# A graph layer kernel: W1's last half in two parts, the node table's rows laid by partitions, a shortened passage and written-out layers

## The chip, the cores and the metric

The kernel runs on one core of a Trainium2 chip. The metric is the device time of one execution in microseconds; lower is better. The time before is 4889.76 us, the median of three runs (4889.51 to 4896.31). The granted TensorE clock of the profiled execution was 0.958 of full speed on average.

## The reference, cut to what matters

The program is one GPS layer on a graph with N = 6250 nodes of 256 features and E = 100000 edges, sorted by destination. Six GNN layers follow one another; then comes a small attention-like term and a feed-forward stage with eight experts.

```python
xn = _layernorm(x, axis=-1)
h = xn
for layer in range(6):                                   # the GNN
    agg = jax.ops.segment_sum(h[src], dst, num_segments=n)
    z = h + agg
    z = z @ W1[layer] + b1[layer]
    z = relu(batchnorm(z, g1[layer], be1[layer]))        # mean and variance over all nodes
    z = z @ W2[layer] + b2[layer]
    z = batchnorm(z, g2[layer], be2[layer])
    h = z if layer == 5 else relu(z)
x = x + h + mix(xn)                                      # 8 heads, k and v normed, kv = k'v / N
x = x + ffn(_layernorm(x))                               # 8 experts: 3 products each, mixed by a softmax
```

Each batch norm needs the mean and the variance over all 6250 nodes, so no row of the next product can start before the last row of the one before is known. Each gather `h[src]` needs the whole table of h. These are the barriers of the program.

## The kernel before, in words

**Data.** 6250 nodes are padded to 6272 = 49 tiles of 128, in NC = 7 chunks of CT = 7 tiles (CN = 896 columns, halves of HN = 448). The state lives transposed in SBUF as `Zt` (features on partitions, nodes as columns, FB = 2 blocks of features). A copy of it by rows lies in DRAM as `y_table` (6272 x 256 fp32, 1 KB a row). Node t*128+p is row t*128+p of it (`y_t`, L102), so a chunk of 7 tiles goes to and from SBUF in pieces of 1 KB.

**Edges.** The 784 tiles of 128 edges are cut into S = 7 sections of 112. The first 50 tiles of each section are gathered: GpSimd issues one indirect DMA for each tile (`gather`, L654) that fetches 128 rows by `idx`. The other 62 are summed by a dense product with an adjacency block, that is built in the first layer and kept in DRAM (`dense_half`, L904). In layers 1 to 5 there are 350 gathers each, in 91 quads of up to four tiles. ScalarE and VectorE split a quad into high and low terms (`quad_high` L1140, `quad_low` L1391), TensorE multiplies it with one-hot matrices (`quad`, L809), VectorE sums a group of quads (`group_rows`, L1487), TensorE transposes it (L817) and VectorE adds it into a window of 128 columns of `Zt` (`add_group`, L1500). Four quads of gathered rows are in flight, so gather n waits until quad n-4 is multiplied. The dense halves lie between the quads in an order written out by hand (`halves_at`, with PRE = 6 halves ahead of the first quad).

**W1.** `w1_half` (L928) multiplies one half chunk (448 columns) with W1. In layers 1 to 5 thirteen of the 14 halves lie among the last quads. The 14th, the first half of chunk 6, waits for the last group and comes after it. ScalarE copies each result back to `Zt` (`evict_z1`, L1160) and VectorE takes its statistics from there (`z1_stats`, `half_stats`, L1519).

**The passage** is what lies between the last gather of a layer and the first of the next:

1. the last group, W1's last half, its eviction and statistics;
2. `bn_coefficients` on VectorE (two `bn_aggr` L1608, then seven small steps L1609 to L1617, each waiting for the one before, with a square root on ScalarE, L1165, in between);
3. ScalarE's `affine` (L1115) of the first half chunk, and `w2_stage` on TensorE: 14 halves, 112 matmul records (L967), evicted by ScalarE (L1174), statistics by VectorE (L1519);
4. `bn_coefficients` again;
5. `rows_of_h`: ScalarE's affine with Relu over all columns (the first chunk in pieces of 4 and 3 tiles), TensorE's transposes (L786), VectorE's 28 copies (`copy_rows`, L1378) into three row buffers `Rb`, and SP's stores to `y_table` (`store_rows`, L512: one for a chunk, two for the last). A copy of chunk c waits until chunk c-3 is stored. GpSimd's `table_complete` holds the first gather until all stores have landed. VectorE then makes the low terms of the first chunk (L1384), and TensorE starts the dense halves with them.

**Loops.** On all engines layer 0 is written out and layers 1 to 5 are one hardware loop over l (`with pe.Fori(1, L)`, `act.Fori`, `dve.Fori`, `pool.Fori`; SP's has l = 1 to 4 and one more). VectorE's loop starts with `layer_parameters` (L1630) and ends with the second `bn_coefficients`. The feed-forward stage runs seven chunks of eight experts; chunks 0 to 5 are a hardware loop on TensorE, ScalarE, GpSimd and VectorE. In each expert step TensorE does two times seven products (`hidden`, L1064) and 28 output products (`outputs`, L1073), VectorE adds products (L1827) and outputs (L1843), and GpSimd forms sums of weights and inputs and adds a biased row for each of seven tiles (L735). At a chunk's last expert it puts `chunk_inputs` (L707 to L713: rel, rest, idx as buffers for the next chunk's inputs) behind its third row.

**The start.** Until about 96 us the kernel norms x, stores the table (ScalarE's queue, seven chunks) and `xn_cols`, and VectorE computes the edge tables in a chain of steps, each waiting for the one before (L1653 to L1741). A flag at its end says whether edges are left for `general_pass`, a slow path that doesn't run with these inputs. The first gather waits for the flag.

```python
W1_ORDER = [*range(HALVES - 2), HALVES - 1, HALVES - 2]      # HALVES = 14
last_ = sections(gb_f)[:, S - 1, 0:GS // PJ]                 # no group of the last section reaches chunk 6's second half
step(tsc(last_, last_, float((NC - 1) * CN + HN - P), None, ALU.min))
```

## Time and profile before

| | us |
|---|---|
| median of 3 runs | 4889.76 (4889.51 to 4896.31) |
| the profiled execution: its own time | 4891.97 |
| its span, first to last instruction | 4889.9 |
| TensorE matmul busy | 4457.0 (91%) |
| GpSimd busy | 3100.2 (63%) |
| VectorE busy | 3051.6 (62%) |
| ScalarE busy | 2636.4 (54%) |
| start until the first gather | 98.3 |
| first gather of layer 0 to first gather of layer 1 | 883.2 |
| first gather of layer 1 to that of layer 5 | 2293.8, or 573.4 a layer |
| first gather of layer 5 to the end of the span | 1614.6 |

Busy shares are means over stages that have different limits. How to read it: the stages repeat, so one layer (here the one whose first gather is at 1554.99 us and whose successor's is at 2128.84 us) is read in full and the others are compared with it. The timelines give for each group of instructions its start, its length in us, engine, source line, operation, tiles and, in brackets, how long its engine stood idle before it and what ended that.

### The profile page before, as it was taken

To read this page: it belongs to the slowest core of one execution; us is meant where nothing else is said; L and a number is where in the kernel's file an instruction comes from. 1 tells how busy PE (TensorE), PEld (TensorE's weight loads), DVE (VectorE), ACT (ScalarE), POOL (GpSimd) and SP (SyncE) were. 2 spreads that over 40 slices of the span, in tenths; PEclk is the share of its full clock that TensorE was granted. 3 is DMA by queue.
4 is the path that set the end of the run, shared out by engine and by line. 5 is a ranking of instruction groups with operands and counts; after the bars stand their busy time and mean duration, and the time that the engine had idled before them with its cause. 6 is when DMAs were issued, how large, how long until landed. Compare 5 with 4: busy or idle time off the path is not lost.

```text
span 4889.9 us, 73690 instructions
## 1 busy us (share of the span) xinstructions
PE 4457.0 (91%) x18751; PEld 3229.0 (66%) x18751; DVE 3051.6 (62%) x6933; ACT 2636.4 (54%) x3302; POOL 3100.2 (63%) x3400
## 2 busy tenths in 40 slices
PE   3899999899987999889997999879998899999999
PEld 2666688477755878467774777547774766666665
DVE  6788766456664666556665566646665566666666
ACT  2677533555645655355555555455564355555555
POOL 1777765077761777447772677717775067777786
PEclk6999999999998999899999999989999899999999
DMA  5444653155533554255542555335555100000000
GB/s 196 135 150 155 218 154 96 63 158 170 157 103 106 167 165 149 65 161 166 159 131 77 166 165 160 113 101 161 164 152 169 60 10 9 9 9 9 9 8 8
DMA packets 248726, 560.54 MB, mean 115 GB/s; under 512 B 44210, under 2 KB 124956, under 8 KB 248156
## 3 DMA queue, kind: packets, MB, share of 16 engines
q0 software_dynamic: 109728, 299.78, 20.8%
q1 hardware_dynamic: 125788, 226.99, 14.1%
q10 hardware_dynamic: 12768, 28.90, 1.6%
q8 instruction: 153, 2.51, 0.2%
q14 instruction: 289, 2.37, 0.2%
HBM read 481.66 MB, written 73.84 MB: 114 GB/s over the span
## 4 chain that ended last, share of the span: by engine, by line
PE 59%; POOL 15%; issue 13%; DVE 5%; DMA 5%; ACT 1%; DVEq 0%; POOLq 0%; ACTq 0%; SPq 0%
PE bank L904 21%; PE bank L1064 11%; POOL G L654 8%; POOL BIG L654 7%; PE bank L1073 6%; PE bank L967 6%; PE bank L809 4%; PE bank L806 4%; DMA G<-y_table,idx 3%; PE bank L852 2%; PE bank L928 1%; DVE Gsp L1391 1%; DMA y_table<-BIG 1%; DVE BIG L1378 1%; DMA BIG<-in_x 1%
## 5 line engine op out<-in xcount | busy, mean ns | idle before, releaser
L654 POOL DMA_INDIRECT G<-y_table,idx x1416 | 1457.0, 1029 | 1132.4 <-DMA y_table<-BIG 553.8
L904 PE MATMUL bank<-Ac,Ych 128*128 128x512 f32 x7644 | 1846.8, 396 | 19.2 <-DVE Ych L1384 19.2
L904 PEld LDWEIGHTS bank<-Ac,Ych 128*128 128x128 f32 x7644 | 1460.2, 191 | 331.9 <-issue 20.4
L654 POOL DMA_INDIRECT BIG<-y_table,idx x870 | 890.4, 1023 | 265.0 <-issue 257.1
L1153 ACT CAST Ac<-BIG 128x2048 fp32r<-128x2048 uint8 (+1 forms) x546 | 912.1, 1686 | 225.9 <-PE bank L904 218.3
L1514 DVE TENSOR_TENSOR Z<-Z,bank 128x512 f32 x546 | 375.3, 687 | 438.6 <-PE bank L904 396.9
L809 PE MATMUL bank<-Gsp,onehot 128*128 128x512 f32 x1750 | 514.7, 415 | 138.8 <-DVE Gsp L1391 137.6
L1400 DVE TENSOR_SCALAR onehot<-iota,rel 128x128 fp32r<-128x128 f32 x2290 | 540.6, 302 | 78.4 <-PE bank L809 48.0
L1827 DVE TENSOR_TENSOR G<-G,bank 128x448 f32<-128x448 f32 x784 | 462.4, 619 | 190.4 <-ACT G L1299 99.6
L809 PEld LDWEIGHTS bank<-Gsp,onehot 128*128 128x128 f32 x1750 | 318.9, 193 | 263.4 <-DVE Gsp L1391 206.7
L1140 ACT CAST Gsp<-G 128x1024 fp32r<-128x1024 f32 (+1 forms) x230 | 232.6, 1011 | 475.0 <-DMA G<-y_table,idx 467.6
L1304 ACT ACTIVATE G<-G,fsh,fsc 128x448 f32<-128x448 f32 x448 | 333.9, 757 | 241.1 <-DVE G L1827 239.2
L1391 DVE TENSOR_TENSOR Gsp<-G,Gsp 128x1024 fp32r<-128x1024 f32 (+1 forms) x230 | 271.2, 1179 | 276.5 <-ACT Gsp L1140 276.1
L1140 ACT CAST Gsp<-BIG 128x1024 fp32r<-128x1024 f32 (+1 forms) x225 | 229.6, 1021 | 392.6 <-DMA BIG<-y_table,idx 387.7
L1391 DVE TENSOR_TENSOR Gsp<-BIG,Gsp 128x1024 fp32r<-128x1024 f32 (+1 forms) x225 | 267.1, 1187 | 168.2 <-ACT Gsp L1140 167.8
L1214 ACT CAST BIG<-bank 128x384 f32 (+2 forms) x672 | 280.4, 512 | 142.4 <-PE bank L852 132.4
L1073 PE MATMUL bank<-BIG,G 128*128 128x256 f32 x1568 | 349.0, 379 | 7.7 <-DVE BIG L1843 5.4
L1519 DVE BATCH_NORM_STATS2 bst<-Z 128x6 f32<-128x448 f32 (+1 forms) x336 | 192.4, 614 | 245.5 <-ACT Z L1174 195.1
L1073 PEld LDWEIGHTS bank<-BIG,G 128*128 128x128 f32 x1568 | 297.4, 190 | 68.3 <-issue 20.4
L967 PE MATMUL bank<-Z,W 128*128 128x448 f32 x672 | 270.0, 566 | 43.4 <-ACT Z L1115 43.4
L806 PE MATMUL bank<-G,onehot 128*128 128x256 f32 x1072 | 265.1, 391 | 26.9 <-DMA G<-y_table,idx 26.9
L928 PE MATMUL bank<-Z,W 128*128 128x448 f32 x672 | 277.7, 561 | 5.0 <-DVE Z L1500 4.0
(212 smaller groups left out, 5278.1 us busy)
## 6 DMA issues: line engine op xcount, KB each, us to landing
BIG<-adjacency SPq DMA_DIRECT2D x273, 448.0 KB, 3.6
y_table<-BIG SPq DMA_DIRECT2D x30, 896.0 KB, 5.6
BIG<-y_table SPq DMA_DIRECT2D x27, 896.0 KB, 6.6
G<-y_table,idx POOLq DMA_INDIRECT x1416
adjacency<-BIG ACTq DMA_DIRECT2D x7, 3136.0 KB
BIG<-y_table,idx POOLq DMA_INDIRECT x870, 2.9
BIG<-in_x SPq DMA_DIRECT2D x14, 896.0 KB, 8.8
y_table<-BIG ACTq DMA_DIRECT2D x7, 896.0 KB, 11.2
```

The lines of the kernel that those rows point to most:

```text
L654: nc.gpsimd.indirect_dma_start(out=rows[:, j, :], out_offset=None, in_=y_table, in_offset=bass.IndirectOffsetOnAxis(ap=idx[:, t:t + 1], ax ...
L806: last = mm(group_bank(g)[:, 0:D], onehot[:, q, j, :].bitcast(fp32), rows[:, j, :], start=start, stop=stop)
L809: last = mm(group_bank(g)[:, 0:2 * D], onehot[:, q, j, :], Gsp[n % RQ][:, j, :, :].rearrange("p k f -> p (k f)"), start=start, stop=stop)
L904: last = mm(bank[2 * (k % 2) + b][:, 0:UW], Ych[pos % 2][:, i, s, b * P:(b + 1) * P], Ac[x_ % NAC][:, i - CA * h, :], start=(i == 0 and s ...
L967: last = mm(bank[2 * h + fo][:, 0:HN], W2[:, b, fo * P:(fo + 1) * P], Zt[:, b, n0:n1], start=(b == 0), stop=(b == FB - 1))
L1064: mm(product_bank(e, second, name)[:, 0:HN], w, x_, start=True, stop=True).then_inc(s_fh, 1)
L1073: last = mm(out_bank(e, k)[:, 0:D], h2T[:, b, k * P:(k + 1) * P], We[:, 2, e, b, :], start=(b == 0), stop=(b == FB - 1))
L1140: nc.scalar.copy(Gsp[n % RQ][:, 0:tiles(n), 0, :], rows[:, 0:tiles(n), :]).then_inc(s_gh, 1)
L1153: nc.scalar.copy(Ac[x_ % NAC][:, 0:t1 - t0, :], Land[k % NL][:, t0:t1, :]).then_inc(s_ac, 1)
L1391: tt(Gsp[n % RQ][:, 0:m, 1, :], gathered(l, n)[0][:, 0:m, :], Gsp[n % RQ][:, 0:m, 0, :].bitcast(fp32), ALU.subtract).then_inc(s_gl, 1)
L1400: last = tsc(onehot[:, n % 2, j, :], iota[:, :], rel[:, t + j:t + j + 1], None, ALU.is_equal)
L1827: tt(to, a, product_bank(e, second, product_)[:, 0:HN], ALU.add).then_inc(s_fv, 1)
```

## The change

Seven things change together.

1. **The table's layout.** Node t*128+p is now row p*49+t of `y_table`. A chunk of 7 tiles is then 7 KB in one piece for each partition. `idx` is rewritten once at the start by GpSimd (`table_rows`: four operations of 128x784, after VectorE's `s_viol` steps), since idx*49 + (idx>>7)*(1-49*128) is the new row. SP stores the rewritten indices to DRAM (`src_rows`) and waits for that before it goes on; the slow path reads them from there. VectorE shifts all 784 columns of idx instead of 434.
2. **Stores.** Chunk 0's store is split into tiles 0-1 and 2-6.
3. **W1's last half in two parts** of 256 and 192 columns (`W1_PARTS` = 15, `LAST_PART` = 5632). The last section's last group is kept from starting below column 5632 (`late`). The part of 256 columns then needs all groups but the last and moves among the quads, at n = 88; only the part of 192 columns stays behind the last group. In layer 0 all 15 parts come at the end.
4. **Statistics from the bank.** The last part's statistics (and the last W2 half's) are taken by VectorE from the PSUM bank as soon as each feature block is done; ScalarE's eviction of that block waits for VectorE.
5. **Fewer steps in `bn_coefficients`:** the addition of epsilon goes into ScalarE's square root (a bias), and the last two steps become one fused operation for each feature block, with no wait between them. W2's first products wait for one feature block of the affine at a time.
6. **`rows_of_h`** has chunk 0 in pieces of 2, 2 and 3 tiles.
7. **Loops.** The layer loop is written out on TensorE, ScalarE and VectorE (GpSimd's and SP's stay), and the feed-forward loop on VectorE (the others' stay). GpSimd's `chunk_inputs` moves one row earlier (k == 2 instead of 3).

```diff
+    FIRST_ROWS = [0, 2, 4, 7]
...
-    y_t = y_table.rearrange("(t p) f -> p t f", p=P)
+    y_t = y_table.rearrange("(p t) f -> p t f", p=P)
+    src_rows = nc.dram_tensor("src_rows", (P, ET), i32).ap()
...
+        W1_PARTS = HALVES + 1
+        LAST_PART = (NC - 1) * CN + 2 * P
...
-        W1_ORDER = [*range(HALVES - 2), HALVES - 1, HALVES - 2]
+        W1_ORDER = [(x_, *half_cols(x_ // 2, x_ % 2), x_ % 2) for x_ in (*range(HALVES - 2), HALVES - 1)]
+        W1_ORDER += [(HALVES - 2, (NC - 1) * CN, LAST_PART, 0), (HALVES - 2, LAST_PART, (NC - 1) * CN + HN, 1)]
...
             def store_rows(l, c):
-                for t0, t1, m in ((0, TA, 2), (TA, CT, YP)) if c == NC - 1 else ((0, CT, YP),):
+                for t0, t1, m in {0: ((0, 2, 1), (2, CT, YP)), NC - 1: ((0, TA, 2), (TA, CT, YP))}.get(c, ((0, CT, YP),)):
...
+            sp.wait_ge(s_map, 4)
+            sp.dma_start(src_rows, idx[:, :]).then_inc(s_sr, LANES)
+            sp.wait_ge(s_sr, LANES)
             stray_indices(0)
...
+            def table_rows():
+                hold(pool, s_viol, N_VIOL)
+                nc.gpsimd.tensor_scalar(brow_f, idx[:, :], float(NT), None, ALU.mult).then_inc(s_map, 1)
+                nc.gpsimd.tensor_scalar(dnx_f, dnx_i, float(1 - NT * P), None, ALU.mult).then_inc(s_map, 1)
+                pool.wait_ge(s_map, 2)
+                nc.gpsimd.tensor_tensor(brow_f, brow_f, dnx_f, ALU.add).then_inc(s_map, 1)
+                pool.wait_ge(s_map, 3)
+                nc.gpsimd.tensor_copy(idx[:, :], brow_f).then_inc(s_map, 1)
+                hold(pool, s_map, 4)
...
                 for k in range(CT):
-                    if k == NSH - 1 and not final and e == X - 1:
+                    if k == 2 and not final and e == X - 1:
                         hold(pool, s_fh, product(n, 0, "p4"))
                         chunk_inputs(c + 1)
...
+                elif i == W1_PARTS - 1:
+                    pe.wait_ge(s_add, groups_before(l) + NGR)
+                elif i == W1_PARTS - 2:
+                    pe.wait_ge(s_add, groups_before(l) + NGR - 1)
...
                         for fo in range(FB):
                             for b in range(FB):
+                                if c == h == fo == 0:
+                                    pe.wait_ge(s_a1, l * (NC + 2) + b + 1)
                                 last = mm(bank[2 * h + fo][:, 0:HN], W2[:, b, fo * P:(fo + 1) * P],
...
-            with pe.Fori(1, L) as l:
+            for l in range(1, L):
...
             def rows_of_h():
-                affine(0, ACT.Relu, s_h, 0, NA)
-                affine(0, ACT.Relu, s_h, NA, CN)
+                for a, b in zip(FIRST_ROWS, FIRST_ROWS[1:]):
+                    affine(0, ACT.Relu, s_h, a * P, b * P)
...
+                    if i == W1_PARTS - 1:
+                        act.wait_ge(s_bst, (l * (W1_PARTS + HALVES) + i) * FB + fo + 1)
+                    last = nc.scalar.copy(Zt[:, fo, n0:n1], z1_bank(h, fo)[:, 0:n1 - n0])
...
-                act.wait_ge(s_bn, n * N_BN + FB + 1)
-                af(bsd[:, :], bve[:, :], ACT.Sqrt).then_inc(s_bnsq, 1)
+                act.wait_ge(s_bn, n * N_BN + FB)
+                af(bsd[:, :], bmv[:, :, 1], ACT.Sqrt, bias=eps_bn[:, 0:1]).then_inc(s_bnsq, 1)
...
+            def bank_stats(k, h, n, there, value):
+                for b in range(FB):
+                    dve.wait_ge(there, value + b + 1)
+                    V.bn_stats(bst[:, b, k, :], z1_bank(h, b)[:, 0:n]).then_inc(s_bst, 1)
...
-                step(tsc(bve[:, :], bmv[:, :, 1], EPS_BN, None, ALU.add))
...
-                step(tt(bsh[:, :], bmu[:, :], bsc[:, :], ALU.mult))
-                tt(bsh[:, :], bsh[:, :], parl[:, o + 2, :], ALU.add).then_inc(s_bnr, 1)
+                for b in range(FB):
+                    last = stt(bsh[:, b:b + 1], bmu[:, b:b + 1], bsc[:, b:b + 1], parl[:, o + 2, b:b + 1], ALU.mult, ALU.add)
+                last.then_inc(s_bnr, 1)
...
+            late = sections(gmin_f)[:, S - 1, TG[GPS - 1] // PJ:GS // PJ]
+            step(tsc(late, late, float(LAST_PART), None, ALU.max))
...
-            step(tsc(sections(shi_i), src_i, 7, None, ALU.arith_shift_right))
+            step(tsc(dnx_i, idx[:, :], 7, None, ALU.arith_shift_right))
...
-            with dve.Fori(1, L) as l:
+            for l in range(1, L):
...
-            with dve.Fori(0, NC - 1) as c:
+            for c in range(NC):
                 for e in range(X):
-                    ffn_step(c, e, False)
-            for e in range(X):
-                ffn_step(NC - 1, e, True)
+                    ffn_step(c, e, c == NC - 1)
```

## Rows read from the trace of the kernel before

**Rows 1.** The page's part 4: the chain that ended last, by engine.

```profile
PE 59%; POOL 15%; issue 13%; DVE 5%; DMA 5%; ACT 1%; DVEq 0%; POOLq 0%; ACTq 0%; SPq 0%
```

**Rows 2.** Line L654, one layer's gathers (1540 to 2040 us), with duration in ns.

```profile
L654 POOL DMA_INDIRECT G<-y_table,idx x176: 942/946/2678, 1555.0 to 2025.1; - x176
...
  issue: 102.0, 335
```

**Rows 3.** Timeline of GpSimd (start, us; idle before): gathers behind that layer.

```profile
2128.84 0.94 POOL L654 DMA_INDIRECT G<-y_table,idx  x1 [100.29 <-DMA y_table<-BIG]
...
2154.68 2.07 POOL L654 DMA_INDIRECT G<-y_table,idx  x1 [6.15 <-PE bank L809]
```

**Rows 4.** Timeline of W1's last half up to W2, same layer.

```profile
2035.66 6.23 PE L928 MATMUL bank<-Z,W 128*128 128x448 f32 x8 [0.61 <-DVE Z L1500]
...
2041.93 0.97 ACT L1160 COPY Z<-bank 128x448 f32<-128x448 f32 x2 [10.89 <-PE bank L928]
...
2042.93 1.15 DVE L1519 BATCH_NORM_STATS2 bst<-Z 128x6 f32<-128x448 f32 x2 [6.54 <-ACT Z L1160]
...
2045.60 0.17 DVE L1609 TENSOR_SCALAR bve<-bmv 128x2 f32<-128x2 f32 x1 [0.16 <-DVE bmv L1608]
...
2047.46 0.16 DVE L1617 TENSOR_TENSOR bsh<-bsh,parl 128x2 f32<-128x2 f32 x1
2047.66 4.76 ACT L1115 ACTIVATE Z<-Z,bsh,bsc 128x448 f32<-128x448 f32 x6 [1.65 <-DVE bsh L1617]
...
2049.12 45.55 PE L967 MATMUL bank<-Z,W 128*128 128x448 f32 x112 [7.23 <-ACT Z L1115]
```

**Rows 5.** Timeline of TensorE: W1's last half in the four other layers.

```profile
1463.04 5.82 PE L928 MATMUL bank<-Z,W 128*128 128x448 f32 x8 [0.61 <-DVE Z L1500]
...
2608.32 4.92 PE L928 MATMUL bank<-Z,W 128*128 128x448 f32 x8 [0.61 <-DVE Z L1500]
...
3183.18 5.92 PE L928 MATMUL bank<-Z,W 128*128 128x448 f32 x8 [0.61 <-DVE Z L1500]
...
3756.90 3.27 PE L928 MATMUL bank<-Z,W 128*128 128x448 f32 x8 [0.61 <-DVE Z L1500]
```

**Rows 6.** Timeline of the end of W2 in the same layer as rows 4.

```profile
2094.71 0.97 ACT L1174 COPY Z<-bank 128x448 f32<-128x448 f32 x2 [2.04 <-PE bank L967]
...
2095.71 1.11 DVE L1519 BATCH_NORM_STATS2 bst<-Z 128x6 f32<-128x426 f32 x2 [1.85 <-ACT Z L1174]
```

**Rows 7.** Timeline of the rows of h and the stores, same layer.

```profile
2100.38 15.03 ACT L1115 ACTIVATE Z<-Z,bsh,bsc 128x512 f32<-128x512 f32 x16 [1.65 <-DVE bsh L1617]
...
2104.01 0.17 DVE L1630 COPY parl<-par 128x12 f32 x1 [3.67 <-issue]
...
2118.53 4.54 DVE L1378 COPY BIG<-bank 128x512 f32<-128x512 f32 x8 [1.40 <-DMA y_table<-BIG]
...
2125.16 21.77 PE L904 MATMUL bank<-Ac,Ych 128*128 128x512 f32 x84 [3.81 <-DVE Ych L1384]
```

**Rows 8.** The same place ahead of layer 1, reached without a jump back.

```profile
954.50 15.02 ACT L1115 ACTIVATE Z<-Z,bsh,bsc 128x512 f32<-128x512 f32 x16 [1.65 <-DVE bsh L1617]
...
967.59 2.22 DVE L1378 COPY BIG<-bank 128x512 f32<-128x512 f32 x4 [0.81 <-DMA y_table<-BIG]
971.17 4.55 DVE L1378 COPY BIG<-bank 128x512 f32<-128x512 f32 x8 [1.37 <-DMA y_table<-BIG]
```

**Rows 9.** Windows: us, busy of PE, PEld, DVE, ACT, POOL, PEclk, DMA share, GB/s.

```profile
2110.00:2120.00 10.00, 6.94 (x47) 4.99 (x48) 7.42 (x14) 8.24 (x8) 0.00 (x0) 1.00 1.02 338
```

**Rows 10.** Waits from 4000 to 4870 us: total, times, longest; then one row's addition.

```profile
PE bank L1073 <- DVE BIG L1843: 5.4, 5, 1.1
...
PE bank L1064 <- POOL idx L713: 4.7, 6, 0.8
...
4059.94 0.73 POOL L735 TENSOR_TENSOR BIG<-BIG,biased 128x256 f32 x1
```

**Rows 11.** Timeline of the edge tables at the start: the narrow shift.

```profile
74.60 0.61 DVE L1699 TENSOR_SCALAR BIG<-idx 128x434 int32<-128x434 int32 x1
```

120 lines of the change are left out of this document (67 added, 53 removed).

## The prediction

> **What bounds the kernel now.** I read the chain that ended last first: TensorE has 59% of it, GpSimd 15%, "issue" 13% [rows 1]. That is a mean over stages, so I then read one layer in full. In a gather stage GpSimd sets the pace. One gather takes 946 ns (median) with 0.30 us between two (102.0 us in 335 gaps) [rows 2]; the 350 of a layer take from 1555.0 to 2028.5, or 1.35 us each. TensorE is full for most of that stage but ends it waiting for rows. After the last gather GpSimd stands idle 100.29 us, until the table is stored [rows 3]. This passage is a chain through all engines, and what shortens it shortens the program, five times with the rows of h and a sixth time without. The feed-forward stage is TensorE's, with small gaps at each chunk's end [rows 10].
>
> So the sum has two sorts of terms: links of the passage, times 5 or 6, and gaps at chunk ends. The gathers' pace is not touched by any edit.
>
> **W1's last half in two parts.** Behind the last group stand 8 matmul records of 448 columns. They took 6.23 us [rows 4] and 5.82, 4.92, 5.92 and 3.27 us in the other layers [rows 5], mean 5.23. The fastest is the 2.4 GHz level (0.41 us a record), the slowest the 1.2 GHz level (0.78). The part of 256 columns moves among the quads, where TensorE waits for rows anyway; its cover is the wait ahead of the last quad. 192 columns in proportion are 1.4 and 2.7 us at the two levels. As the weights are no smaller I take 2.5 us as the mean: 2.7 x 5 = 13.6 us (10 to 15). Layer 0 gains nothing here.
>
> **Statistics from the bank.** TensorE ends at 2041.89, ScalarE copies both blocks, VectorE's statistics end at 2044.08 [rows 4]: 2.19 us. In the new order the first block's statistics lie beside the second block's matmuls; left are one of 192 columns (0.58 us for 448, so 0.25) and a hand-over of 0.2. Saved 1.7 x 6 = 10.2 us (8 to 11). ScalarE's eviction waits for VectorE now, but its next work is the square root, which comes over 1 us later. For W2's last half TensorE ends at 2094.67 and the statistics at 2096.82 [rows 6], 2.15 us; a block of 426 columns is 0.55, so about 0.7 stay: 1.4 x 6 = 8.6 us (7 to 9).
>
> **Fewer steps.** From 2045.60 to 2047.46 VectorE starts six steps 0.31 us apart [rows 4]. One goes (0.31); the fused last pair needs no wait between its operations (0.2). The square root starts 0.3 earlier and stays hidden behind two steps. 0.51 us x 12 norms = 6.1 us (4 to 7).
>
> **W2 by feature blocks.** ScalarE starts at 2047.66, TensorE at 2049.12 [rows 4]: two affines of one half. With one needed it starts 0.68 earlier, and its first matmuls take longer than the second affine. 0.68 x 6 = 4.1 us (0 to 4.5).
>
> **The rows of h.** ScalarE's affine starts at 2100.38, the last copies end at 2118.53 + 4.54 = 2123.07: 22.7 us [rows 7]. Two things stretch it. VectorE, at its loop's end, stands 3.67 us in "issue" before its first instruction at 2104.01 [rows 7]; ahead of layer 1, reached without a jump, the same stretch is 975.72 - 954.50 = 21.2 us [rows 8], so the jump costs 1.5, four times. And the copies wait for stores that must free their row buffers: 0.81 + 1.37 us [rows 8]. The DMA engines are full then, share 1.02 at 338 GB/s [rows 9]: a chunk of 917 KB takes 2.7 us there, while VectorE copies one in 2.2 us [rows 8]. Splitting chunk 0 lets the first copy start some 0.6 us earlier (two tiles of affine instead of four, of 15.0 us for 49) and the stores some 2 us earlier; long packets help further. I take both stalls as gone: 21.2 - 2.2 - 0.6 + 0.2 = 18.6 us after the affine's start. That saves 4.1 us four times and 2.6 once: 19.0 us. Bounds: the jump, the earlier start and a third of the stalls alone give 10; GpSimd's earlier start counted too gives 25.
>
> Why not count the first gather's full gain, which may be 6 us a layer? After the first gathers GpSimd waits 6.15 us for the first quad's product and goes on at 2154.68 [rows 3]. That wait hangs on TensorE, which started at 2125.16 behind VectorE's low terms and so behind the copies [rows 7]. An earlier store only makes that wait longer.
>
> **Long packets by themselves.** The stores' DMA time shortens by an unknown share; nothing in the rows moves such packets. They take part in the stalls above, which the earlier start nearly covers, in the landing of the last store, which is not what comes last, and in the start, where loads and stores share the DMA engines: seven chunks of 2.7 us, 15% less, on three legs of the chain: 1.2 us gained (0 to 2.7). By the Trainium skill, "DMA: Bandwidth & Descriptors", section "Specifications", a transfer is at line rate from 512 B up, so that pieces of 1 KB lose nothing and pieces of 7 KB gain nothing; the sum would then be 1 to 6 us smaller.
>
> **The start.** On VectorE the shift grows from 0.61 us [rows 11] to 1.1, and one step of 0.3 is added: 0.8 us lost. GpSimd's four operations of 784 columns, at 0.73 us for 256 [rows 10], are at most 2.2 us each, 9 together. They run beside VectorE's chain, which has 19 us to go until the flag, and SP's store and wait lie in the same cover; if that cover were gone they would cost some 13 us. What they cost VectorE I can't read: nothing to 9 us, I take 3. The Trainium skill, "SBUF — State Buffer", section "SBUF: two separate sides", says that GpSimd and VectorE exclude each other on a shared port for a whole instruction; by that the cost would be nearer to 6 or 7. The start then loses 0.8 + 3 - 1.2 = 2.6 us.
>
> **Feed-forward.** TensorE waits 5.4 us, five times, for VectorE's outputs at a chunk's end [rows 10], where VectorE jumps; with what follows I take 1.3 us each, 6.5. It waits 4.7 us, six times, for GpSimd's last input (L713) [rows 10]. One row's addition less ahead of it is 0.73 us [rows 10]: 4.4. Together 10.9 us (5 to 12). ScalarE's and GpSimd's jumps stay; next late is TensorE itself.
>
> **Written-out loops elsewhere.** TensorE's and ScalarE's jumps lie under waits for each other: 0 us. Code is fetched in order as in the first layer, which shows no such stall in its gather stage: 0, at worst 1 us a layer.
>
> **Sum.** 13.6 + 10.2 + 8.6 + 6.1 + 4.1 + 19.0 + 10.9 - 2.6 = 69.9 us. The profiled span is 4889.9, its execution's own time 4891.97, the median of the runs 4889.76, so the span stands for the median: 4889.8 - 69.9 = 4819.9, say 4820 us, 1.4% less.
>
> **Rivals.**
> *The clock joins in.* Each gap of the passage is followed by a stretch at 1.2 GHz; the same 8 records took 3.27 us or 6.23 us by luck [rows 4, 5]. The gap ahead of W2 shrinks from 7.23 [rows 4] to about 4.3 us. If TensorE keeps the high level there and at W1's tail, W2's first 6 us lose half, 3 us x 6, and the tail 1 us x 5: some 20 us more, 4800 us. For it: the 3.27. Against it: idle gaps of that size remain. 0.2.
> *The rows of h keep their length.* TensorE's transposes or the stores limit them after all, and only the jump and the smaller piece count: 10 instead of 19, 4829 us. 0.12.
> *Slower: the gathers' pace.* 1750 gathers at 1.35 us carry the program. If loads in pieces of 7 KB, or the table's new order, make gathers come back or be issued later, each 0.01 us costs 17.5 us. From 0.04 us a gather on (3%) the gain is gone; at 0.05 the time is 4907 us. Against it: the row that is fetched is 1 KB as before, only 4 loads a layer are changed, and GpSimd's pace hangs on issue, not on landing [rows 2]. 0.03.
> *It doesn't do what it says.* If the raised start of the last group leaves an edge out of its window, the slow path runs in each layer, and it is slower by far. A window of 128 nodes stands some 30 nodes clear on each side by the mean of 16 edges a node. 0.01.
> *Forecast:* 0.64.
>
> **Range and chances.** Adding the lower bounds of all terms gives a gain of 40 us, the upper ones 85, neither likely at once. Against 4820 I take 4798, so that most of the clock's case is inside, to 4842. 0.2% or 9.8 us is about what a measurement of this kernel can tell from no change. Faster by more 0.95, within 0.02, slower by more 0.03.
>
> **What would show it.** Last gather to first gather near 86 us instead of 101 (the first gather gains more than the layer does). The layer's period near 562 us instead of 573. VectorE's last copy 18.6 us after the affine's start, with no wait for a store. W1's last part 1.5 to 3 us. The gathers' pace still 1.35 us. Gaps at chunk ends gone in the feed-forward stage. The first gather at about 101 us. I am wrong if the pace moves, if GpSimd no longer waits for the first quad's product, or if VectorE stalls in written-out code.

## The result, and the profile after the change

| | before, us | changed, us | ratio [95% interval] |
|---|---|---|---|
| first comparison | 4889.6 (4889.2 to 4896.3) | 4847.4 (4836.0 to 4850.8) | 0.9906 [0.9888, 0.9925] |
| again_2 | 4896.2 (4890.9 to 4906.7) | 4843.8 (4839.2 to 4850.4) | 0.9888 [0.9874, 0.9903] |
| again_4 | 4903.7 (4901.6 to 4909.5) | 4848.9 (4843.0 to 4863.2) | 0.9893 [0.9875, 0.9912] |

The rows again_2 and again_4 are repetitions of the comparison. The change makes the kernel 42 to 55 us faster, 0.9 to 1.1%. I had forecast 70 us (4820, range 4798 to 4842). The direction was right, and the first comparison lies 5 us outside my range. The traced execution of the changed kernel is its fastest (4836.0, span 4834.3), so its trace shows 56 us of gain. Two more traces of the changed kernel have spans of 4848.6 and 4841.3, and a second one of the kernel before 4899.6. Against one trace each, the differences below would hold scatter too; so I use the means of two traces before and three after: 4894.7 and 4841.4, which is 53.3 us.

Again the chain that ended last, by engine. It has hardly moved [rows 1], so it can't tell where the time went:

```profile
PE 61%; POOL 15%; issue 12%; DVE 6%; DMA 4%; ACT 2%; POOLq 0%; DVEq 0%; ACTq 0%; SPq 0%
```

The passage can. GpSimd's timeline behind the same layer as in [rows 3] (start, us; in brackets the idle time before and what ended it):

```profile
2106.97 0.94 POOL L678 DMA_INDIRECT G<-y_table,idx  x1 [90.08 <-DMA y_table<-BIG]
...
2125.71 1.74 POOL L678 DMA_INDIRECT BIG<-y_table,idx  x1 [0.30 <-issue]
2130.74 2.07 POOL L678 DMA_INDIRECT G<-y_table,idx  x1 [3.29 <-PE bank L837]
```

100.29 us of idle time became 90.08. The wait for the first quad's product is still there, so what counts is the moment at which the gathers resume, here 2130.74. From W1's last part to W2 (answers rows 4):

```profile
2024.75 2.93 PE L960 MATMUL bank<-Z,W 128*128 128x192 f32 x8 [0.61 <-DVE Z L1542]
2026.44 0.37 DVE L1566 BATCH_NORM_STATS2 bst<-bank 128x6 f32<-128x192 f32 x1 [0.96 <-PE bank L960]
2027.72 0.72 ACT L1198 COPY Z<-bank 128x192 f32<-128x192 f32 x2 [8.43 <-PE bank L960]
2027.72 0.37 DVE L1566 BATCH_NORM_STATS2 bst<-bank 128x6 f32<-128x192 f32 x1 [0.91 <-PE bank L960]
...
2030.88 0.35 DVE L1668 SCALAR_TENSOR_TENSOR bsh<-bmu,bsc,parl 128x1 f32<-128x1 f32 x2
2031.26 4.76 ACT L1150 ACTIVATE Z<-Z,bsh,bsc 128x448 f32<-128x448 f32 x6 [1.44 <-DVE bsh L1668]
...
2032.07 5.34 PE L1001 MATMUL bank<-Z,W 128*128 128x448 f32 x7 [4.39 <-ACT Z L1150]
```

The statistics start where TensorE ends a block (2027.72), beside the copy and not behind it, and TensorE is idle for 4.39 us instead of 7.23. The end of W2 and the copies of rows (answers rows 6 and 7):

```profile
2076.91 0.61 DVE L1566 BATCH_NORM_STATS2 bst<-bank 128x6 f32<-128x426 f32 x1 [0.35 <-PE bank L1001]
...
2080.64 4.30 ACT L1150 ACTIVATE Z<-Z,bsh,bsc 128x256 f32<-128x256 f32 x7 [1.44 <-DVE bsh L1668]
...
2082.94 0.69 DVE L1420 COPY BIG<-bank 128x512 f32<-128x512 f32 x1 [2.12 <-PE bank L814]
2083.93 0.69 DVE L1420 COPY BIG<-bank 128x512 f32<-128x512 f32 x1 [0.29 <-PE bank L814]
2085.12 1.02 DVE L1420 COPY BIG<-bank 128x512 f32<-128x512 f32 x2 [0.50 <-PE bank L814]
2087.17 0.69 DVE L1420 COPY BIG<-bank 128x512 f32<-128x512 f32 x1 [1.03 <-PE bank L814]
2088.03 12.26 DVE L1420 COPY BIG<-bank 128x512 f32<-128x512 f32 x23 [0.16 <-PE bank L814]
```

In this passage no copy waits for a store, and no "issue" stall precedes the first. (In the passage behind layer 3 one still does, shown further down.) But the copies end at 2100.3, 19.65 us after the affine's start, and not at 18.6: they wait 0.29 + 0.50 + 1.03 us for transposes, which TensorE makes at its low clock level here and for which it waits 0.51 us for the affine, and the other 23 run at VectorE's own pace, 0.53 us each.

TensorE's waits in the feed-forward stage, 4000 to 4820 us (answers rows 10: total, times, longest):

```profile
PE bank L1098 <- ACT G L1341: 3.3, 6, 0.5
PE bank L1107 <- ACT G L1346: 2.3, 1, 2.3
PE bank L1098 <- POOL idx L738: 2.3, 6, 0.4
```

The wait for VectorE is gone (5.4 us), that for GpSimd halved (4.7 to 2.3), and one for ScalarE is new (3.3 in six times; the single one of 2.3 us stands in both kernels).

The stages, in us. A passage is what lies between the last gather of a layer and the resumed gathers of the next; sums over the layers it occurs in:

| stage | before | changed | difference | forecast |
|---|---|---|---|---|
| start to first gather | 98.4 | 101.3 | +2.9 | +2.6 |
| last gather to W1's end, 5 layers | 66.2 | 50.6 | -15.6 | -13.6 |
| W1's end to W2's start, 6 | 43.4 | 26.7 | -16.7 | -17.3 |
| W2, 6 | 269.1 | 268.9 | -0.2 | 0 |
| W2's end to the next affine or stage, 6 | 36.5 | 24.9 | -11.6 | -11.7 |
| affine to resumed gathers, 5 | 268.3 | 253.6 | -14.7 | -19.0 |
| resumed to last gather, 5 | 2242.2 | 2242.5 | +0.3 | 0 |
| layer 0's gathers | 726.6 | 729.4 | +2.7 | 0 |
| mixing stage | 107.6 | 111.4 | +3.8 | 0 |
| feed-forward | 954.7 | 950.4 | -4.3 | -10.9 |

(The forecast's statistics, 10.2 and 8.6, with half of the 6.1 us of fewer steps each, and W2 by blocks, 4.1, stand in the third and the fifth row.) The rows add up to 53.4 us, the spans differ by 53.3. What the rows leave out is equal in both kernels: W1 in layer 0 (74.3 us) and the 7.5 us behind the last matmul. Of the rows only the gather stages scatter by themselves: "resumed to last gather" was 2232, 2251 and 2244 us in the three traces of the changed kernel. What I had named as signs: the layer's period is 562.3 us in the mean of three traces (forecast 562, before 573.8), and from a layer's last gather to the next first one it takes 86.2 to 91.0 us (forecast 86, before 96.8 to 101.2).

### The profile page after: what moved, and what is told of

Read it like the earlier page. It is cut to its first block, busy times and chain, and to the rows that moved or that the text cites. A ratio compares the mean times of both kernels' runs of the same rounds, so it can differ in the third digit from the quotient of the medians.

```text
span 4834.3 us, 68084 instructions
## 1 busy us (share of the span) xinstructions
PE 4440.0 (92%) x18799; PEld 3229.9 (67%) x18799; DVE 3050.6 (63%) x6934; ACT 2643.0 (55%) x3324; POOL 3104.8 (64%) x3405
## 3 DMA queue, kind: packets, MB, share of 16 engines
q1 hardware_dynamic: 79676, 227.39, 13.7%
## 4 chain that ended last, share of the span: by engine, by line
PE 61%; POOL 15%; issue 12%; DVE 6%; DMA 4%; ACT 2%; POOLq 0%; DVEq 0%; ACTq 0%; SPq 0%
PE bank L932 23%; PE bank L1098 11%; POOL G L678 9%; PE bank L1107 6%; PE bank L1001 6%; POOL BIG L678 6%; PE bank L837 5%; PE bank L834 4%; DMA G<-y_table,idx 3%; PE bank L880 2%; PE bank L960 1%; DVE Gsp L1433 1%; DVE BIG L1420 1%; ACT Gsp L1176 1%; DMA BIG<-in_x 1%
## 5 line engine op out<-in xcount | busy, mean ns | idle before, releaser
L932 PE MATMUL bank<-Ac,Ych 128*128 128x512 f32 x7644 | 1833.9, 394 | 18.9 <-DVE Ych L1426 18.9
L1107 PEld LDWEIGHTS bank<-BIG,G 128*128 128x128 f32 x1568 | 299.0, 191 | 61.6 <-issue 20.4
L1001 PE MATMUL bank<-Z,W 128*128 128x448 f32 x672 | 269.1, 565 | 26.7 <-ACT Z L1150 26.7
L880 PE MATMUL bank<-BIG 128*128 128x408 bf16 (+1 forms) x1302 | 261.5, 331 | 21.4 <-ACT BIG L1254 13.2
```

The source lines that it names most:

```text
L932: last = mm(bank[2 * (k % 2) + b][:, 0:UW], Ych[pos % 2][:, i, s, b * P:(b + 1) * P], Ac[x_ % NAC][:, i - CA * h, :], start=(i == 0 and s ...
L1001: last = mm(bank[2 * h + fo][:, 0:HN], W2[:, b, fo * P:(fo + 1) * P], Zt[:, b, n0:n1], start=(b == 0), stop=(b == FB - 1))
L1107: last = mm(out_bank(e, k)[:, 0:D], h2T[:, b, k * P:(k + 1) * P], We[:, 2, e, b, :], start=(b == 0), stop=(b == FB - 1))
```

## The experiments

Ratios are to runs of the kernel before beside them. On two chips the kernel before took 5391 and 5442 us and not 4890 to 4904; runs there are told with that number.

**The two kernels again.** The changed kernel without an edit.

> The changed kernel once more, to see whether its runs scatter (4836.0 to 4850.8 so far, the kernel before 4889.2 to 4896.3). If the four times seen are one broad distribution, the new times fall between 4834 and 4852 with no gap. If the traced execution differs from the untraced ones (by where the clock falls, or because the first execution is the fast one), all untraced ones lie at 4845 to 4851 and the traced one near 4836. The trace's last W1 part ends 10.9 to 11.7 us after the last gather in each of five layers, as in the first trace.

Run again. Kernel before 5391.2, changed 5312.6 (5300.0 to 5327.5), 0.9855 [0.9832, 0.9877]. This was another chip, so the question of the scatter stayed open, and a new one came up; the expected 10.9 to 11.7 us from the last gather to W1's end were 16.0 us on average here. The same layer's gather stage, from its first gather to its last, there and in the changed kernel's first trace (windows: length, then busy time with counts of PE, PEld, DVE, ACT, POOL, granted clock, DMA share, GB/s), first the chip at 5391:

```profile
1746.90:2282.80 535.90, 472.02 (x1865) 362.75 (x1864) 287.72 (x613) 261.31 (x214) 370.45 (x350) 0.92 0.44 132
```

```profile
1542.10:2016.90 474.80, 449.48 (x1876) 349.15 (x1875) 290.81 (x615) 264.51 (x216) 361.90 (x350) 0.98 0.49 149
```

The stage is 61 us longer. VectorE and ScalarE have nearly the same busy time and GpSimd 9 us more; TensorE is idle for 64 us instead of 25, and busy for 23 us more at a granted clock of 0.92 instead of 0.98. The difference sits where gathers run: a chunk of the feed-forward stage takes 134.3 us on both, and W2 and the way from the affine to the first gather take the same. What delays TensorE there was not settled. Stages outside the gathers could be compared on either chip.

> The changed kernel a third time, beside the three below. If this chip is of the first sort (the kernel before near 4889), 4836 to 4851 again; if it is of the second (before near 5391, TensorE stalling in the gather stages of every kernel), 5300 to 5328. In both the passages from last to first gather are 88 to 97 us.

Run again_2. 4843.8 (4839.2 to 4850.4) against 4896.2: 52 us faster, as expected; from last to first gather it took 86 to 90 us, a little less than the 88 to 97 expected.

> The changed kernel once more, as the partner of the run below. On a chip of the first sort: 4836 to 4858 us; stages as before: W1's end to W2's start 4.4 us, a chunk of the feed-forward stage 134.3 us, the mixing stage 110.3 to 110.7 or 113.2 us, the resumed gathers 49.5 to 52.5 us after the affine's start.

Run again_3. 5363.5 (5343.7 to 5376.7) against 5442.4, 0.9849 [0.9811, 0.9887]: a chip of the other sort.

> The changed kernel as the partner of the run below. First sort of chip: 4836 to 4858 us; slow sort: 5300 to 5380. From the resumed gathers to the last one 443 to 454 us a layer on the first sort, 499 to 512 on the slow one.

Run again_4. 4848.9 (4843.0 to 4863.2) against 4903.7: 55 us faster. The expectation held for the median and for the gathers, though one run took 4863.

> The kernel before once more, for a second trace of it. If its stages reproduce as those of the changed kernel do: W1's end to W2's start 7.2 us, W2's end to the next stage 8.0, VectorE's last copy 21.2 to 22.7 us after the affine's start, a chunk of the feed-forward stage 135.4 us. Open are the stages that scattered in the changed kernel: from the resumed gathers to the last one 443 to 454 us a layer, the gather stage of layer 0 724.7 us in the one trace of before against 726.8 to 732.4, the mixing stage 107.6 against 110.3 to 113.2. If before shows 729 and 110 here too, these differences are none of the change's; if it shows 725 and 107 again, the change costs 5 and 3 us there.

Run before_again. One time, 4901.7; the kernel before, beside it, had a median of 4904.4 and 4893.0 to 4917.9. So scatter of 15 us belongs to both kernels, and no cause of the change's is needed for it. In the trace layer 0's gathers took 728.6 us (724.7 in the first), so that difference is scatter; the mixing stage took 107.56 us (107.57), so that one is the change's.

**The order of rows.** The changed kernel with the old order:

```diff
-    y_t = y_table.rearrange("(p t) f -> p t f", p=P)
+    y_t = y_table.rearrange("(t p) f -> p t f", p=P)
...
-            sp.wait_ge(s_map, 4)
-            sp.dma_start(src_rows, idx[:, :]).then_inc(s_sr, LANES)
-            sp.wait_ge(s_sr, LANES)
...
-            table_rows()
             gather_stage(0)
```

> The changed kernel with the table's rows in the old order (tile by tile, packets of 1 KB again), without the four GpSimd operations and the store ahead of the first gather. Theory 1 (the scatter comes from the new order: gathers that hit rows laid out differently, or long packets beside loads): the runs lie within 2 us of each other, and the median is below the changed kernel's, near 4838. Theory 2 (the scatter is that of written-out code or of the clock): it scatters as before, and the median is above the changed kernel's by the stores' longer packets time in five passages, 1 to 8 us, less the 3 us that the start wins back: 4846 to 4853. By my forecast the start's first gather moves from 101.5 to about 98.7 us, and the rows of h get longer by 0.5 to 1.5 us a layer.

Run old_order, on the chip at 5391: 5303.4 (5299.4 to 5307.0), 0.9834 [0.9815, 0.9853], 9 us below the changed kernel with intervals that overlap. The times decide for neither theory; these runs spread over 8 us, those of the changed kernel beside them over 28.

> The rows in the old order again, beside again_2. Theory 1 (the new order costs: start, and loads and gathers that disturb each other): 5 to 10 us below the changed kernel on either sort of chip, 4838 to 4842 on the first, and with runs within 2 us there. Theory 2 (the new order gives what I forecast): 1 to 8 us above it. A difference inside 3 us either way says that the new order is worth nothing.

Run old_order_2. 4851.2 (4850.8 to 4854.5), 0.9909 [0.9895, 0.9923], 7 us above again_2, inside theory 2's 1 to 8. The intervals of the times overlap, so what follows rests on the traces. First gather at 98.0 us, 3.1 earlier. The copies of the same passage as above:

```profile
2091.92 8.74 DVE L1415 COPY BIG<-bank 128x512 f32<-128x512 f32 x16 [0.57 <-PE bank L810]
2101.11 2.22 DVE L1415 COPY BIG<-bank 128x512 f32<-128x512 f32 x4 [0.45 <-DMA y_table<-BIG]
2103.82 2.22 DVE L1415 COPY BIG<-bank 128x512 f32<-128x512 f32 x4 [0.49 <-DMA y_table<-BIG]
```

The waits for stores are back although the first chunk is still split: 6.2 us in five passages, against 1.4 to 2.1 in the three traces of the changed kernel and 12.6 in that of before. The resumed gathers come 52.0 us after the affine's start (mean of five) against 50.7, so the order is worth 1.3 x 5 - 3.1 = 3.4 us in the changed kernel.

The kernel before with the new order alone (the same edit the other way, with the four GpSimd operations):

> The kernel before with the table's rows laid by partitions alone (with the remapping of indices on GpSimd and the store). My forecast: the start loses 3 to 4 us, long packets give 1.2 and perhaps 0.5 us in each of five passages: 4889 + 0 to +3, so 4888 to 4893. Theory 1 (the new order scatters): its runs spread over 10 us or more. A page-like rule of line rate from 512 B would give plus 3 to 4, 4893. If the gathers' pace moved with the order, the length of a gather stage of 350 (472.6 us mean before) would change by more than 3 us in every layer.

Run before_new_order. 5370.0 (5364.5 to 5380.4) against 5391.2, 0.9955 [0.9937, 0.9972]: 21 us faster, where I had expected no change or 3 us more. The runs spread over 16 us, those of before beside them over 29, so the scatter doesn't need the new order.

> The kernel before with the new order of rows alone, on a chip of the first sort if it is one. From the traces so far: start 3.0 us later, first gather 3 us earlier in each passage, but the resumed gathers only 1.2 us earlier, so -3 + 5 x 1.2 = 3 us gained, 0.9994 of before. On the other chip it came out 21 us faster and there the changed kernel lost nothing by having it taken away; if that was real, the gain here is 10 us or more, if it was scatter, within 5 us.

Run before_new_order_2. 4894.8 (4882.5 to 4905.9) against 4904.4, 0.9976 [0.9965, 0.9986]: 7 to 17 us faster, where I had expected 3. In its trace the start loses 2.4 us and the resumed gathers come 51.8 us after the affine's start, where the kernel before has 53.7: 1.8 x 5 - 2.4 = 6.8 us, just below that interval's end. So the new order, whose long packets I had priced at 1.2 us by themselves, gives several times that. It gives it in the passages alone: the 2.4 us lost at the start are the 2.2 us by which VectorE's steps are stretched there (below) and 0.2 us of a slower copy, so that nothing was gained on the start's loads and stores. The gathers' pace did not move: 449.1 us from the resumed to the last gather for five layers on average (449.3 and 447.6 in the two traces of before). From its issue to its landing a chunk's store took 5.6 us in the kernel before, 4.6 with the new order alone, and 3.8 in the changed kernel (issues of that size, KB each, median us):

```profile
y_table<-BIG SPq DMA_DIRECT2D x30, 896.0 KB, 5.6
```

```profile
y_table<-BIG SPq DMA_DIRECT2D x30, 896.0 KB, 4.6
```

```profile
y_table<-BIG SPq DMA_DIRECT2D x25, 896.0 KB, 3.8
```

That the packets themselves are faster is shown by a window in which the DMA engines are full, to be held against 338 GB/s at a share of 1.02 [rows 9]; changed kernel:

```profile
2097.00:2101.00 4.00, 1.76 (x14) 1.23 (x12) 4.00 (x8) 4.00 (x4) 0.00 (x0) 1.00 1.01 411
```

**The first chunk in three pieces.** Undone:

```diff
-    FIRST_ROWS = [0, 2, 4, 7]
+    FIRST_ROWS = [0, 4, 7]
...
-                for t0, t1, m in {0: ((0, 2, 1), (2, CT, YP)), NC - 1: ...
+                for t0, t1, m in {NC - 1: ...
```

> The changed kernel with the first chunk of the rows of h in two affines (4 and 3 tiles) and one store, as before. By my forecast 0.6 us of the later first copy and most of the two store stalls (2.2 us) come back, 2.8 us in each of five passages: 14 us slower. Rival (long packets and written-out code alone did it): 3 us or less slower, as the first copy starts 0.6 us later and no store is waited for.

Run whole_first_chunk. 4849.4 (4832.6 to 4853.3), 0.9896 [0.9880, 0.9913], beside 4843.8 of again_2: no difference that these runs can tell, and 14 us is outside what the traces allow. The copies of the same passage:

```profile
2083.27 0.69 DVE L1420 COPY BIG<-bank 128x512 f32<-128x512 f32 x1 [2.55 <-PE bank L814]
2084.12 0.69 DVE L1420 COPY BIG<-bank 128x512 f32<-128x512 f32 x1 [0.16 <-PE bank L814]
2084.98 1.02 DVE L1420 COPY BIG<-bank 128x512 f32<-128x512 f32 x2 [0.16 <-PE bank L814]
2086.53 13.05 DVE L1420 COPY BIG<-bank 128x512 f32<-128x512 f32 x24 [0.52 <-PE bank L814]
```

The first copy starts 0.4 us later and then waits 0.84 us for transposes instead of 1.82 (1.98 with the one of 0.16). With the split the first copy starts earlier, but the extra piece makes ScalarE finish the second chunk's affine 0.56 us later (5.32 us after the affine's start, 4.76 without). Resumed gathers: 50.4 us after the affine's start against 50.7. The split is worth nothing, and the rival that I named holds: the stalls for stores stay small here (3.3 us in five passages), while they grow when the order (6.2 us, above) or the loops (5.5 us, below) are taken back.

**Statistics from the bank.** Undone:

```diff
-                if i < W1_PARTS - 1:
-                    dve.wait_ge(s_z1e, l * W1_PARTS + i + 1)
-                    part_stats(i, n0, n1)
-                else:
-                    bank_stats(i, h, n1 - n0, s_z1, (l * W1_PARTS + i) * FB)
+                dve.wait_ge(s_z1e, l * W1_PARTS + i + 1)
+                part_stats(i, n0, n1)
```

and the same for W2's last half, with ScalarE's two waits for s_bst taken out.

> The changed kernel with the statistics of W1's and W2's last part taken from the copied block, as before, and no wait of ScalarE for them. By my forecast 1.7 + 1.4 us come back in each of six layers, less what the shorter last part makes of it (a block of 192 columns is copied and read in less time, so about 1.2 + 1.4): 15 to 19 us slower. Rival (ScalarE's wait for VectorE gives the gain back): within 3 us.

Run stats_after_copy. 4859.8 (4846.8 to 4865.6), 0.9921 [0.9905, 0.9936], 16 us above again_2, within the 15 to 19 expected; the rival falls. TensorE's gap ahead of W2:

```profile
2033.31 2.92 PE L960 MATMUL bank<-Z,W 128*128 128x192 f32 x8 [0.61 <-DVE Z L1537]
2036.27 0.54 ACT L1195 COPY Z<-bank 128x192 f32<-128x192 f32 x2 [7.49 <-PE bank L960]
2036.85 0.62 DVE L1555 BATCH_NORM_STATS2 bst<-Z 128x6 f32<-128x192 f32 x2 [2.81 <-ACT Z L1195]
...
2041.45 9.05 PE L1001 MATMUL bank<-Z,W 128*128 128x448 f32 x18 [5.22 <-ACT Z L1150]
```

5.22 us in every layer, against 4.39 in layers 1 to 5 and 4.69 in layer 0; from W2's end to the affine 5.27 against 3.77. So reading the bank is worth 4.7 us ahead of W2 and 1.50 x 6 = 9.0 us behind it, 13.7 us.

**The size of W1's last part.** One number changed:

```diff
-        LAST_PART = (NC - 1) * CN + 2 * P
+        LAST_PART = (NC - 1) * CN + P
```

> The changed kernel with W1's last part at 320 columns instead of 192 (the raised start of the last group at the first tile's end instead of the second's). By my forecast 128 columns cost 128/256 of 2.7 us in five layers: last gather to W1's end 1.4 us longer at the low clock and 0.8 at the high one, and the statistics of a block 0.16 longer, twice: 1 to 1.7 us a layer, 5 to 9 us in all. Rival (the part waits for its last group's columns, not for its own length): nothing, last gather to W1's end stays at 8.9 or 10.9 us.

Run last_part_320. 4854.7 (4852.5 to 4857.6) against 4904.4, 0.9901 [0.9886, 0.9916]; the changed kernel was not run beside it, and 50 us of gain is not to be told from its 42 to 55. Last gather to W1's end takes 12.5 to 13.1 us in all five layers. The part itself, and two layers of again_2 with 192 columns, one at each of the clock's levels:

```profile
2028.81 4.45 PE L960 MATMUL bank<-Z,W 128*128 128x320 f32 x8 [0.61 <-DVE Z L1542]
```

```profile
1466.08 1.57 PE L960 MATMUL bank<-Z,W 128*128 128x192 f32 x8 [0.61 <-DVE Z L1542]
...
2032.97 2.93 PE L960 MATMUL bank<-Z,W 128*128 128x192 f32 x8 [0.61 <-DVE Z L1542]
```

The part costs its own length: 2.93 us for 192 columns at 1.2 GHz, 4.5 for 320, 5.8 to 6.2 for 448 [rows 4, 5]. At 2.4 GHz it is 1.57 for 192 and 3.27 for 448. At the low level 320 columns cost 1.5 us more than 192, where I had expected 1.4, and the rival falls. The sum over five layers is 63.4 us against 50.6, so 12.8 us more and not the 5 to 9 expected, because here no layer's part ran at the high level.

**GpSimd's row.** `k == 2` back to `k == NSH - 1` (3), all else changed.

> The changed kernel with GpSimd's inputs of the next chunk behind the third row's addition again (k == 3). By my forecast TensorE waits 0.73 us longer at each of six chunk ends, 134.3 + 0.7 = 135.0 us a chunk. Rival: ScalarE's piece, for which TensorE waits 0.54 us in the changed kernel and not before, takes the whole gain: the wait for GpSimd is 0.78 us instead of 0.38, that for ScalarE 0.1 or less, and a chunk stays within 0.2 of 134.3 us.

Run gpsimd_row_back. TensorE's waits from 4000 to 4830 us:

```profile
PE bank L1098 <- POOL idx L738: 6.4, 6, 1.1
```

One wait of 1.1 us instead of two of 0.4 and 0.5 (the rival had said 0.78); a chunk takes 134.3 us without the edit and 134.4 with it. The rival took the whole gain. With VectorE's loop in place the edit brings nothing either: a chunk takes 135.4 us in the kernel before and in loops_back_3 below, which has it. (One time, 4857.7, within the scatter.)

**Loops instead of written-out code.**

```diff
-            for l in range(1, L):
+            with dve.Fori(1, L) as l:
...
-            for c in range(NC):
+            with dve.Fori(0, NC - 1) as c:
```

and the layer loops of TensorE and ScalarE likewise.

> The changed kernel with the layer loops of TensorE, ScalarE and VectorE and VectorE's loop over the last stage's chunks as loops again. Theory 2 (written-out code is what scatters): the runs lie within 2 us, at 4836 + 1.5 x 4 + 0.9 x 5 = 4846 or a little above. Theory 1 (the new order scatters): they scatter by 10 us or more, at a median of 4847 + 10.5 = 4858. The rows of h then take 1.5 us longer in layers 2 to 5 than ahead of layer 1, and TensorE waits for VectorE at five chunk ends again, 1.1 us each.

Run loops_back. 5337.4 (5333.2 to 5359.3) against 5391.2, 0.9911 [0.9888, 0.9934]; 25 us above again. The runs spread over 26 us, so the scatter doesn't need written-out code either.

> The changed kernel with the layer loops of TensorE, ScalarE and VectorE and VectorE's loop over the last stage's chunks as loops again. By my forecast's prices, corrected by the traces: a chunk of the last stage 135.4 instead of 134.3 us (5 us in all), the resumed gathers of four passages 1.3 to 1.5 us later after the affine's start (52 instead of 50.6): 5 to 6 us; together 10 to 12 us slower than again_3. Rival (written-out code is worth more, as the 25 us on the slow chip say): 20 us or more, with the surplus inside the gather stages, whose resumed part would be longer than 455 us in several layers. Rival (worth only the last stage's part): 5 us, with the resumed gathers at 50.6 us in all passages.

Run loops_back_2. 5402.9 (5397.3 to 5411.8) against 5442.4, 0.9920 [0.9889, 0.9951]; 39 us above again_3, so the rival of 20 us or more holds here. From the resumed to the last gather the five layers took 2574 us against 2543, so on these chips most of it does lie in the gather stages.

> The loops of layers and of the last stage's chunks restored, as before. On the first sort of chip: a chunk of the last stage 135.4 instead of 134.3 us (5 us in all); VectorE's last copy 22 us after the affine's start instead of 19.6 in four passages, 8 to 9 us; together 13 to 14 us slower than again_4, and the resumed part of the gather stages unchanged at 443 to 454 us (rival: longer by 4 to 6 us a layer, as on the slow chips, then 33 to 44 us slower in all). On the slow sort: 25 to 40 us slower, two thirds of it in the gather stages.

Run loops_back_3. 4851.9 (4848.0 to 4856.3) against 4903.7, 0.9889 [0.9872, 0.9905]; 3 us above again_4, where the two intervals together leave room for some 12 either way. The 13 to 14 us expected don't show in the times. The resumed part of the gathers is the same (2242 and 2244 us), chunks of the last stage take 135.4 us. The passage behind layer 2:

```profile
2093.83 0.17 DVE L1685 COPY parl<-par 128x12 f32 x1 [4.74 <-issue]
2094.26 8.59 DVE L1420 COPY BIG<-bank 128x512 f32<-128x512 f32 x16 [0.26 <-DVE parl L1685]
2103.04 2.22 DVE L1420 COPY BIG<-bank 128x512 f32<-128x512 f32 x4 [0.18 <-DMA y_table<-BIG]
2106.38 4.35 DVE L1420 COPY BIG<-bank 128x512 f32<-128x512 f32 x8 [1.13 <-DMA y_table<-BIG]
```

VectorE stands 4.74 us at the jump, and the late copies then wait for stores again. The gathers resume 52.9 us after the affine's start in these four passages, against 50.7. By the traces the written-out code is worth 2.2 x 4 + 1.0 x 5 = 14 us; the spans differ by 11.1, the medians by 3. So this price rests on the traces, one against three.

## Why the prediction was right or wrong

**W1's last half in two parts: right.** 15.6 us instead of 13.6. The part shrank nearly in proportion to its columns (2.93 us at the low level where I had 2.7, 1.57 at the high one where I had 1.4). At equal level last gather to W1's end became 3.1 us shorter (14.1 to 11.0) at the low one and 2.1 (11.0 to 8.9) at the high one. The other 2 us fit the clock: over three traces W1's last part ran at 2.4 GHz in 6 of 15 cases, before in 2 of 10. Over all traces on these chips it is 15 of 40 with 192 columns and 2 of 15 with 448; what sets the level no run shows, so this part of the gain is luck as far as the forecast goes. That much of the rival "the clock joins in" is true; the rest isn't, W2 takes 44.8 us in both kernels although the gap ahead of it shrank to 4.39 us.

**Statistics, fewer steps, W2 by blocks: right.** 28.3 us of 29.0. In the traces W1's end to the end of its statistics shrank by 1.78 us (forecast 1.7), the same behind W2 by 1.50 (1.4), the coefficients by 0.41 and 0.44 (0.51), and TensorE follows ScalarE's affine 0.65 us earlier (0.68). Only the name of one part was wrong: of the 1.78 us reading the bank is 0.83 (the run above), the rest comes from a part of 192 columns being copied and read in less time. The steps and the blocks were not taken back in a run of their own.

**The rows of h: 14.7 instead of 19.0, and for another reason.** The step that failed is "Splitting chunk 0 lets the first copy start some 0.6 us earlier ... and the stores some 2 us earlier", with "I take both stalls as gone: ... 18.6 us". The first copy starts 0.4 us earlier, and the extra piece of the affine takes that back. The stalls for stores shrink from 12.6 us in five passages to 1.4 to 2.1, by the new order and by the missing jump.

At the last copy, which is what I had added up, the gain is smaller still: 22.0 us after the affine's start became 19.9 (mean of 15 passages), 10.6 us in all, which is the number of the rival that named 10. The other 4 us lie between the last copy and the resumed gathers (31.7 became 30.9 us); no run tells which edit gave them. Two things went wrong in my number. I had read one passage as typical, with 22.7 us, and it was the longest of ten. And my floor of 18.6 us took the copies as free of TensorE and of stores. Two passages of the changed kernel, the ten microseconds behind the affine's start: with TensorE at the low level throughout, and with the level back up after some 5 us (windows: length, busy of PE, PEld, DVE, ACT, POOL, clock, DMA share, GB/s):

```profile
955.10:965.10 10.00, 8.28 (x36) 7.21 (x37) 5.47 (x10) 10.00 (x13) 0.00 (x0) 0.50 0.48 178
```

```profile
1521.40:1531.40 10.00, 7.66 (x47) 5.99 (x48) 6.51 (x13) 10.00 (x13) 0.00 (x0) 0.83 0.58 231
```

TensorE does 36 operations instead of 47, nearly all of them transposes, and VectorE 10 instead of 13; the last copies end 20.4 and 18.9 us after the affine's start. Ten of the 15 passages wait for no store: three end at 18.9 us with the level back early, four at 20.4 with it back late, three at 19.6 between. The passage behind layer 3 ends at 20.5 us in all three traces, with the level back early, and waits for a store:

```profile
2661.62 2.22 DVE L1420 COPY BIG<-bank 128x512 f32<-128x512 f32 x4 [1.26 <-DMA y_table<-BIG]
```

The term "long packets by themselves", 1.2 us, was mis-sized: 3.4 us net in the changed kernel and 6.8 in the kernel before, the start's loss of 3.1 and 2.4 us taken off already. Its 15% for the start stood on no row, and the start showed none of it.

**The feed-forward stage: 4.3 instead of 10.9, the largest miss.** Two steps failed. For VectorE's loop I took 1.3 us a chunk, more than the 1.08 us for which TensorE waits [rows 10]; the chunk got 1.0 us shorter (135.4 to 134.4). And "next late is TensorE itself" was wrong. With VectorE and GpSimd earlier, ScalarE's piece is next, 0.54 us behind, so GpSimd's row brings nothing (4.4 us forecast). The upper bound of a removed wait is that wait; what is left of it is set by the second-latest supplier, which the trace of before does not name.

**The mixing stage: 3.8 us lost, not forecast.** Its first 114 matmul records, before and changed (windows: length, PE busy, clock, DMA share, GB/s):

```profile
3820.10:3838.00 17.90, 14.56 (x114) 0.91 0.16 54
```

```profile
3765.30:3785.90 20.60, 17.25 (x114) 0.78 0.14 47
```

The same work takes 2.7 us more at a mean granted clock of 0.78 instead of 0.91, of the 2.9 us that this trace loses; again_2 loses 5.6, which makes the mean 3.8. The gap ahead of it is 1.9 us shorter, so that the stage begins sooner but spends more of its start at 1.2 GHz. All three traces with the old passage (two of before, before_new_order_2) have 107.6 us, all nine on these chips with the new one 110.2 to 113.2. But the gap's length doesn't decide alone: stats_after_copy has a gap of 7.52 us, nearly the old 7.97, and 110.7 us. What puts the low level where it is stays open.

**The start: right in sum, by errors that cancel.** 2.9 us for 2.6. I had 0.8 for the shift and a step, 3 for GpSimd and 1.2 gained by long packets. Measured are 2.2 us for GpSimd and some 0.5 for the step and a slower copy; the shift cost nothing, and long packets gained nothing. What I could not read, VectorE's steps beside GpSimd's operations:

```profile
80.55 2.19 POOL L663 TENSOR_SCALAR BIG<-BIG 128x784 f32<-128x784 int32 x1
82.82 1.83 POOL L665 TENSOR_TENSOR BIG<-BIG 128x784 f32<-128x784 f32 x1
84.72 1.09 POOL L667 CAST idx<-BIG 128x784 int32<-128x784 f32 x1
```

```profile
80.86 0.97 DVE L1771 TENSOR_SCALAR BIG<-rel 128x784 f32<-128x784 f32 x1
81.97 0.98 DVE L1772 SCALAR_TENSOR_TENSOR BIG<-rel,BIG 128x784 f32<-128x784 f32 x1
83.10 2.03 DVE L1773 TENSOR_TENSOR BIG<-BIG 128x434 f32<-128x434 f32 x1
85.27 1.00 DVE L1776 TENSOR_TENSOR BIG<-BIG 128x420 f32<-128x420 f32 x1
```

In the kernel before L1771, L1773 and L1776 took 0.57, 0.61 and 0.60 us; together they lose 2.2 us to 7.3 us of GpSimd's work. The shift got no longer (0.57 us at 784 columns, 0.61 at 434).

**The rest.** The gathers' pace didn't move, the general pass didn't run: both rivals fell. Forecast 69.9, minus 6.6 (feed-forward), 4.3 (rows of h), 3.8 (mixing), 2.7 (layer 0's gathers, within their scatter of 724.7 to 732.4) and 1.1 (small differences of the start, W1 to W2 and the rest), plus 2.0 (W1's part), makes the 53.4 us of the traces. The first comparison shows only 42, but its interval reaches from 37 to 55; the two later ones show 52 and 55. So the middle was 17 us too low by the terms above, and scatter decided that the first median fell outside the range (53 us of gain would have been 4836, inside it). The range was too narrow for both: I gave the measurement itself no share, though medians of the same kernel, each against its neighbour, gave gains from 42 to 55 us, and the lower bounds of all terms with the start's worst case (0.8 + 9) add up to 34 us and not to 40.

## What to carry to other kernels

Before a gap is booked as a gain, ask which supplier would be second; where two edits work on one wait, book the wait once. A first piece cut smaller starts the next engine earlier, but helps only if the pieces behind it keep up. Take the pieces of a passage from traces of several executions: its fixed parts, as W1's end to W2's start, repeated within 0.1 us, while a gather stage of 450 us varied by 11 us and would have passed for a cause.

## What the runs showed of the hardware

**Packet length.** With the DMA engines full, packets of 1 KB moved 338 GB/s [rows 9] and packets of 7 KB 411 GB/s (the window above; each size is 99% of its window's bytes). Over the whole traces the median packet of the stores' and loads' queue took 46 ns for 1 KB in the kernel before and 272 ns for 7 KB in the changed one, 22 and 26 bytes a ns. That speaks against the rule that I had quoted from the Trainium skill, "DMA: Bandwidth & Descriptors", section "Specifications", by which pieces of 1 KB lose nothing: here they lose some 18%.

**GpSimd beside VectorE.** 7.3 us of GpSimd's work stretched VectorE's by 2.2 us in the three steps above, and steps of 784 columns with two inputs kept their 0.98 us. The Trainium skill, "SBUF — State Buffer", section "SBUF: two separate sides", would have VectorE shut out for a whole instruction; the trace shows less than that. Two of the three steps fit it: L1773 and L1776 end 0.48 and 0.46 us after the GpSimd operation beside them, as if held until its end, 1.4 and 0.4 us later than alone. But L1771 ends 0.9 us before GpSimd's L663 does, and L1772, with two inputs, lies beside the same operation and loses nothing.

**Chips differ.** The same kernel took 4890 to 4904 us on some chips and 5391 and 5442 on others, all of it where gathers run, and the changed kernel gained 1.5% there instead of 0.9 to 1.1. The gathers' packets of 4 KB took the same median of 159 ns on both. The cause was not found.
